# A graph network on one core: the last stage written out without a loop, its moments kept per tile, roots and reciprocals taken for four tiles at a time

## What is computed

```python
x = _layernorm(x + _L0_gnn_ref(x, ..., edge_index), axis=-1)
x = _layernorm(x + _L1_gnn_ref(x, src, dst, ...), axis=-1)

# in _L1_gnn_ref, at its end:
S = agg[:, :2 * F] @ (W1_s / np.sqrt(2 * F))
V = jnp.einsum('nmi,mc->nci', agg[:, 2 * F:8 * F].reshape(n, 2 * F, 3), W1_v) / np.sqrt(2 * F)
S = shifted_softplus(S)                    # softplus(x) - log 2
S = S @ (W2_s / np.sqrt(C))                # C = 128
V = jnp.einsum('nci,cd->ndi', V, W2_v) / np.sqrt(C)
return jnp.concatenate([S, V.reshape(n, 3 * C)], axis=1)

def _layernorm(x, axis=-1, eps=1e-05):
    m = jnp.mean(x, axis=axis, keepdims=True)
    v = jnp.var(x, axis=axis, keepdims=True)
    return (x - m) / jnp.sqrt(v + eps)
```

## Time and profile before

| | |
|---|---|
| time, median of 3 runs | 1854.98 us (1854.6 to 1856.04) |
| the profiled execution: time | 1854.7 us |
| its span in the profile | 1853.0 us |
| busy over the span: PE, DVE, ACT, POOL | 75%, 65%, 53%, 57% |
| granted clock of PE over the span, and in the tile turns of `touched` | 0.849, and 0.50 (1.2 GHz) |
| last POOL instruction of the kernel | starts 1846.41 us |

### The profile page before, as it was taken

One profiled execution on the slowest core, in us unless ns is written; L12 is line 12 of the kernel. 1 busy time (PEld: TensorE's weight loads), 2 busy tenths in 40 slices (PEclk: granted clock), 3 DMA queues, 4 the chain that ended last, 5 costly groups with the idle time before them and its releaser, 6 DMA issues. The chain is left out here.

```text
span 1853.0 us, 27588 instructions
## 1 busy us (share of the span) xinstructions
PE 1396.9 (75%) x8180; PEld 1204.7 (65%) x8180; DVE 1206.3 (65%) x3308; ACT 982.5 (53%) x1960; POOL 1048.5 (57%) x1095
## 2 busy tenths in 40 slices
PE   4669599999968999996699999353333239999833
PEld 4558488888856888885588888242232128888722
DVE  6575466666637777763699997464444239999865
ACT  3743144444425777762566664385656634444476
POOL 4773757777534787774423320577777744333236
PEclk8995699999987999998799999566655569999955
DMA  2000556666545766753555552888786532233112
GB/s 58 2 2 1 151 196 222 218 223 220 192 161 205 260 250 241 252 200 143 212 180 220 210 185 107 257 279 271 256 267 234 200 118 84 88 90 91 52 62 112
DMA packets 98920, 313.66 MB, mean 169 GB/s; under 512 B 34576, under 2 KB 36064, under 8 KB 98802
## 3 DMA queue, kind: packets, MB, share of 16 engines
q0 software_dynamic: 62720, 183.99, 29.5%
q1 hardware_dynamic: 36082, 128.24, 19.6%
HBM read 161.18 MB, written 156.39 MB: 171 GB/s over the span
## 5 line engine op out<-in xcount | busy, mean ns | idle before, releaser
L851 PE MATMUL ps_b<-yhi,whi 128*128 128x500 f32 x960 | 390.3, 407 | 8.6 <-DVE ylo L718 8.6
L851 PE MATMUL ps_b<-yhi,wlo 128*128 128x500 f32 x960 | 375.2, 391 | 0.0
L851 PE MATMUL ps_b<-ylo,whi 128*128 128x500 f32 x960 | 374.9, 390 | 0.0
L795 ACT COPY aggT<-ps_b 128x500 f32<-128x500 f32 x240 | 137.9, 574 | 347.1 <-PE ps_b L851 347.1
L747 DVE BATCH_NORM_STATS2 stat<-aggT 128x6 f32<-128x500 f32 x240 | 163.2, 680 | 200.4 <-ACT aggT L795 198.3
L635 POOL DMA_INDIRECT rows<-rows_out,node_at x160 | 187.0, 1169 | 118.3 <-ACT rows_out L800 82.7
L1068 PE MATMUL fin_ps_x<-ident,fin_X 128*127 128x128 f32 (+1 forms) x320 | 75.4, 405 | 176.9 <-DVE fin_xr L1000 163.4
L851 PEld LDWEIGHTS ps_b<-yhi,whi 128*128 128x128 f32 x960 | 182.5, 190 | 40.1 <-DVE ylo L718 9.1
L851 PEld LDWEIGHTS ps_b<-yhi,wlo 128*128 128x128 f32 x960 | 181.4, 189 | 37.8
L851 PEld LDWEIGHTS ps_b<-ylo,whi 128*128 128x128 f32 x960 | 182.4, 190 | 30.8
L1068 PEld LDWEIGHTS fin_ps_x<-ident,fin_X 128*127 128x127 f32 (+1 forms) x320 | 65.8, 298 | 192.8 <-DVE fin_xr L1000 169.2
(11 more groups left out here) (344 smaller groups left out, 3319.8 us busy)
## 6 DMA issues: line engine op xcount, KB each, us to landing
z<-aggT SPq DMA_DIRECT2D x60, 1000.0 KB, 5.3
X<-z SPq DMA_DIRECT2D x40, 1000.0 KB, 5.3
fin_X<-z SPq DMA_DIRECT2D x20, 1000.0 KB, 6.8
rows<-rows_out,node_at POOLq DMA_INDIRECT x160, 3.1
own_row<-in_L_gnn_W SPq DMA_DIRECT2D x2, 1024.0 KB, 10.6
others<-ord_nodeid,ord_place_node POOLq DMA_INDIRECT x80, 2.1
R<-in_x,node_at POOLq DMA_INDIRECT x80, 3.6
G<-rows,srci POOLq DMA_INDIRECT x80, 5.3
```

Of the source, the lines that this page charges most:

```text
L795: nc.scalar.copy(f.aggT[t % 2][:, j, :], f.ps_b[j % 2][:, 0:COLS]).then_inc(x["copied"], 1)
L851: o = nc.tensor.matmul(f.ps_b[j % 2][:, 0:COLS], w[:, c, j * P:(j + 1) * P], y[b % 2][:, c, :], start=(c == 0 and i == 0), stop=(c == C - ...
```

## The change

In `touched`, and nowhere else but for the sizes of its tiles:

- No loop: each engine's 40 turns are written out, with constant waits and slices.
- PE reads `l.sT` directly (L1467 and `l.hb` go), starts with the first of the four parts of the shifted sum and has four banks instead of two.
- DVE writes the moments of all 40 tiles to one tile `l.mv` (128 x 40 x 2) with no wait for a buffer; reciprocal and product are taken once for four tiles (`GS = 4`), after tile b with b % 4 = 1 of the next group. Each instruction has its wait right ahead of it.
- ACT takes the root of four tiles at once, one group ahead of the scalings.
- POOL reads the column of `l.row` directly (L1490 and `l.idx2` go).

```diff
-    RING = 8
+    RING, GS, parts = 8, 4, 4
+    NG, per = ET // GS, ET // parts
...
+    group = [slice(g * GS, (g + 1) * GS) for g in range(NG)]
...
         @block.scalar
...
-            act.wait_ge(s["plus"], parts)
-
-            def body(t):
-                if t.runs(3):
-                    b, q = t.block(3), t.slot(3, 2)
-                    ge(act, s["prod"], b - 1)
-                    nc.scalar.copy(l.hb[q][:], l.sT[:, bass.ds(P * b, P)]).then_inc(s["hcopy"], 1)
-                if t.runs(0):
-                    b, q = t.block(), t.slot(0, 2)
-                    act.wait_ge(s["aggr"], b + 1)
-                    nc.scalar.activation(l.std[q][:], l.mv[q][:, 1:2], ACT.Sqrt, bias=k.eps[:, 0:1]).then_inc(s["root"], 1)
-                if t.runs(-1):
-                    b, q, r = t.block(-1), t.slot(-1, 2), t.slot(-1, RING)
-                    act.wait_ge(s["nmr"], b + 1)
-                    ge(act, put[r], 16 * t.round(-1, RING))
-                    nc.scalar.activation(l.Y[r], x_row(b), ACT.Identity, scale=l.rstd[q][:], bias=l.nmr[q][:]).then_inc(s["done"], 1)
-            run(act, body)
+
+            def root(g):
+                act.wait_ge(s["aggr"], GS * (g + 1))
+                nc.scalar.activation(l.std[:, group[g]], l.mv[:, group[g], 1], ACT.Sqrt, bias=k.eps[:, 0:1]).then_inc(s["root"], 1)
+
+            root(0)
+            for g in range(NG):
+                if g + 1 < NG:
+                    root(g + 1)
+                act.wait_ge(s["nmr"], g + 1)
+                for b in range(GS * g, GS * g + GS):
+                    ge(act, put[b % RING], 16 * (b // RING))
+                    nc.scalar.activation(l.Y[b % RING], l.X[:, b, :], ACT.Identity,
+                                         scale=l.rstd[:, b:b + 1], bias=l.nmr[:, b:b + 1]).then_inc(s["done"], 1)
...
         @block.gpsimd
...
-                    ge(pool, s["idx2"], b + 1)
-                    ge(pool, s["done"], b + 1)
-                    ge(pool, put[r_next], 16 * t.round(0, RING))
-                    if t.runs(0):
-                        nc.gpsimd.tensor_copy(l.idx2[r_next][:], l.row[:, bass.ds(b + 1, 1)]).then_inc(s["idx2"], 1)
-                    pool.indirect_dma_start(out_dram, bass.IndirectOffsetOnAxis(ap=l.idx2[r][:, 0:1], axis=0), l.Y[r], None,
-                                            bounds_check=m.N - 1, oob_is_err=False).then_inc(put[r], 16)
...
+            for b in range(ET):
+                ge(pool, s["done"], b + 1)
+                pool.indirect_dma_start(out_dram, bass.IndirectOffsetOnAxis(ap=l.row[:, b:b + 1], axis=0), l.Y[b % RING], None,
+                                        bounds_check=m.N - 1, oob_is_err=False).then_inc(put[b % RING], 16)
...
         @block.tensor
...
+            for b in range(ET):
+                pe.wait_ge(s["plus"], b // per + 1)
+                ge(pe, s["ysum"], b - 3)
+                nc.tensor.matmul(l.ps[b % 4][:, 0:P], l.sT[:, P * b:P * (b + 1)], l.W2s[:], start=True, stop=True).then_inc(s["prod"], 1)
...
         @block.vector
...
+            def scales(g):
+                dve.wait_ge(s["root"], g + 1)
+                nc.vector.reciprocal(l.rstd[:, group[g]], l.std[:, group[g]]).then_inc(s["rec"], 1)
+                dve.wait_ge(s["rec"], g + 1)
+                nc.vector.scalar_tensor_tensor(l.nmr[:, group[g]], l.mv[:, group[g], 0], -1.0, l.rstd[:, group[g]],
+                                               ALU.mult, ALU.mult).then_inc(s["nmr"], 1)
...
+            for b in range(-2, ET):
+                if b + 2 < ET:
+                    dve.wait_ge(s["prod"], b + 3)
+                    nc.vector.tensor_tensor(l.X[:, b + 2, 0:P], l.X[:, b + 2, 0:P], l.ps[(b + 2) % 4][:, 0:P], ALU.add).then_inc(s["ysum"], 1)
+                if 0 <= b + 1 < ET:
                     dve.wait_ge(s["ysum"], b + 2)
...
+                    ge(dve, s["aggr"], b)
+                    nc.vector.bn_stats(l.st[(b + 1) % 2][:], l.X[:, b + 1, :]).then_inc(s["stats"], 1)
+                if b >= 0:
                     dve.wait_ge(s["stats"], b + 1)
...
+                    nc.vector.bn_aggr(l.mv[:, b, :], l.st[b % 2][:]).then_inc(s["aggr"], 1)
+                    if b % GS == 1 and b >= GS:
+                        scales(b // GS - 1)
+            scales(NG - 1)
```

More of the change, by code:

```diff
@@ L1431, in touched @@
 def touched(m, k, l, out_dram):
-    nc, ET = m.nc, m.ET
+    nc, ET, D = m.nc, m.ET, m.D
     mag = l.rows[:, 0:m.EPAD]
-    names = ("mag", "exp", "log", "pos", "plus", "vec", "hcopy", "prod", "ysum", "stats", "aggr", "root", "rec", "nmr", "done", "idx2")
+    names = ("mag", "exp", "log", "pos", "plus", "vec", "prod", "ysum", "stats", "aggr", "root", "rec", "nmr", "done")
     s = {n: m.sem(f"tch_{n}") for n in names}
-    RING = 8
+    RING, GS, parts = 8, 4, 4
+    NG, per = ET // GS, ET // parts
     put = [m.sem(f"tch_put{r}") for r in range(RING)]
-    parts = 4
     part = [slice(i * m.EPAD // parts, (i + 1) * m.EPAD // parts) for i in range(parts)]
[L1443 to L1447, removed]
+    group = [slice(g * GS, (g + 1) * GS) for g in range(NG)]
     with nc.Block() as block:
@@ L1518, in _, with plus @@
             dve.wait_ge(s["pos"], parts)
-            for i in range(parts):
+            def plus(i):
                 dve.wait_ge(s["log"], i + 1)
@@ L1522, in _ @@
                                                ALU.add, ALU.add).then_inc(s["plus"], 1)
-            def body(t):
-                b = t.block()
-                if t.runs(1):
+            def scales(g):
[4 more added lines that the diff above has]
+                                               ALU.mult, ALU.mult).then_inc(s["nmr"], 1)
@@ L1528, in body @@
+            for i in range(parts):
+                plus(i)
+            for b in range(-2, ET):
[3 more added lines that the diff above has]
+                if 0 <= b + 1 < ET:
                     dve.wait_ge(s["ysum"], b + 2)
-                if t.runs(0):
+                    ge(dve, s["aggr"], b)
+                    nc.vector.bn_stats(l.st[(b + 1) % 2][:], l.X[:, b + 1, :]).then_inc(s["stats"], 1)
+                if b >= 0:
@@ L1530, in body @@
                     dve.wait_ge(s["stats"], b + 1)
[L1531 to L1547, removed]
-                    nc.vector.scalar_tensor_tensor(l.nmr[q][:], l.mv[q][:, 0:1], -1.0, l.rstd[q][:], ALU.mult, ALU.mult).then_inc(s["nmr"], 1)
@@ L1549, in _ @@
-            run(dve, body)
+                    nc.vector.bn_aggr(l.mv[:, b, :], l.st[b % 2][:]).then_inc(s["aggr"], 1)
+                    if b % GS == 1 and b >= GS:
+                        scales(b // GS - 1)
+            scales(NG - 1)
 class Bag:
@@ L1698, in build @@
             l.dot = m.sb("l_dot", [P, P])
-            l.st, l.mv = two("st", [P, 6]), two("mv", [P, 2])
-            l.std, l.rstd, l.nmr = (two(n, [P, 1]) for n in ("std", "rstd", "nmr"))
+            l.st, l.mv = two("st", [P, 6]), m.sb("l_mv", [P, ET, 2])
+            l.std, l.rstd, l.nmr = (m.sb(f"l_{n}", [P, ET]) for n in ("std", "rstd", "nmr"))
             l.Y = [g[:, 4 * h:4 * h + 4, :].rearrange("p a b -> p (a b)") for g in l.msg + l.agg for h in range(2)]
```

5 lines of the change are left out of this document (removed).

## The result

The changed kernel takes 1842.83 us (median of 4 runs, 1841.96 to 1843.39) beside 1854.79 of the kernel before (1854.13 to 1856.04): a ratio of 0.9934, 95% interval 0.9917 to 0.9952, 12.0 us less. It was run again later beside 15 runs of the kernel before: 1844.14 (1842.79 to 1844.88) to 1854.54, 0.9945, 0.9931 to 0.9958, 10.4 us less.

A forecast was written before the change was run, and what follows sets the result against it. A ring of DVE, ACT's copy and PE paced the last stage, POOL following; afterwards POOL paces. 14.5 us gained by pace less 4.4 lost at the start took 1854.7 to 1844.6, by the median 1844.9 us; range 1843.3 to 1849.5.

The forecast's parts named there:

- The bound before: Last stage: DVE, ACT's copy and PE wait in a ring, 1.67 us per tile; POOL follows with room.
- POOL at 1.28 us per write afterwards: Last stage after the change: POOL's writes pace, 39 steps of 1.28 us make 49.9, 14.5 us gained by the pace.
- ring and DMA have room: Last stage: eight output tiles need 4.9 of the 10.2 us that eight writes take; DMA share rises to 0.43.
- The start: Last stage: scaling waits for the moments of tile 7, so first write at 1786.4 against 1781.99, 4.4 us lost.
- p: DVE's time per tile for add, bn_stats and bn_aggr, without the scales: bounds 0.89 and 1.17 us, 1.03 taken.
- the 0.78: Time in us from the end of ACT's first scaling to the start of POOL's first write in the last stage.
- DVE slower than its starts say: Rival, last stage: DVE takes about 1.35 us per tile and starves POOL by groups; 1851.9 us, chance 6%.
- POOL's instruction grows beside a denser DVE: Rival, last stage: POOL's write takes 1.17 us, 1.47 with issue, as in the layers; 1852.3 us, chance 6%.
- Slower, because the gap belongs to the wait: Rival, last stage: POOL's idle time before each write stays without the copy, pace 1.65 us; 1859.4 us, chance 4%.
- No effect: Rival, last stage: an unseen wait, say the four banks, keeps the ring closed; 1855 us, chance 2%.

The follow-up runs named there:

- loops_out: The kernel before with the last stage's 40 turns written out instead of a loop, nothing else changed: 1852.24 us, ratio 0.9987.
- out_nohb: The kernel before with turns written out, TensorE reading `l.sT` directly over four banks and starting earlier, POOL's index copy kept: 1844.68 us, ratio 0.9948.
- out_nopoolcopy: The kernel before with turns written out and POOL's index copy and its waits removed: 1852.39 us, ratio 0.9988.
- after_skip: The changed kernel with every place marked as skipped, so the last stage's writes carry no rows: 1844.27 us, ratio 0.9945.
- after_poolcopy: The changed kernel with POOL's index copy put back ahead of each write: 1846.18 us, ratio 0.9953 to the kernel before.
- after_ring4: The changed kernel with a ring of four output tiles instead of eight: 1843.82 us, ratio 0.9947 to the kernel before.
- after_stats2: The changed kernel with a second, unused bn_stats per tile on DVE: 1855.75 us, ratio 1.0007 to the kernel before.
- after_gs1: The changed kernel with groups of one tile, a root and a reciprocal for each: 1838.41 us, ratio 0.9918 to the kernel before.

## Why the prediction missed its range by 0.5 us

**The bound before** (a ring of DVE, ACT's copy and PE, POOL a follower): right. loops_out and out_nohb landed 0.6 and 1.0 us under their numbers, with the steps as expected, out_nopoolcopy gave nothing.

**POOL at 1.28 us per write afterwards:** right to the last digit that the profile gives, 49.9 us for 39 steps. That it holds with rows and with none (after_skip), that a copy adds 0.06 (after_poolcopy) and that ring and DMA have room (after_ring4, after_skip) came out as worked out.

**The start** is the term that was mis-sized. I had the first write 30.6 us after the stage's start (1786.4 less 1755.8), it came at 29.54: 4.4 us lost were forecast, 3.35 measured. The step that failed is the choice of p. The starts in the earlier trace rows gave 0.89, the one step with a wait 1.17, and I took the middle, 1.03, "since the new order has no wait ahead of the add but four waits per tile to issue". It was 0.88, with those waits in place. So waits that are already met cost DVE nothing here; the 1.17 held an idle time of 0.20 that came from waiting for the bn_aggr just ahead, and the new order has no such wait. Seven tiles at 0.15 too much are 1.05 us. Against that, a scaling to its first write took 0.93 us (1782.01 + 0.81 to 1783.75), not the 0.78 that I took from another stage in the earlier trace rows; the rest of the sum was right to 0.2.

**The range** had no term for the stages ahead of the change. With p at its lower bound the sum gave 1843.6, and the stage's 11.2 us off 1854.98 give 1843.8, inside the range: p alone does not carry the forecast out of it. The stage's 11.2 us off the medians beside which the changed kernel ran give 1843.6 and 1843.3; measured were 1842.83, 0.8 us less, and 1844.14, 0.8 us more. With the stage itself the same to 0.05 us, this is put down to the stages ahead. Only the profiled executions show them: they put the start of this stage anywhere within 2.3 us. Whether a first median lands 0.8 us to one side or the other is chance. A range for a median of a few runs has to include that spread, here about 1 us to each side.

**The rivals.** DVE slower than its starts say: wrong, it was as fast as them. The mechanism is real: after_stats2 shows it, with 0.59 us more per tile. POOL's instruction grows beside a denser DVE: wrong. Its ground was weak as well: where the 160 longer writes stand, DVE was busy for 58 to 72% of each 200 us (122.76, 115.83, 143.92 and 135.31, from 200 to 1000), no denser than the 67 and 73% of the tile turns before. What lengthened them stays open. Between 1776 and 1800 DVE was busy 23.80 of 24 us, and the writes of that stretch took 0.97 us except the first two, with 1.01 and 1.00. By the rule of the Trainium skill (SBUF — State Buffer, section Who interferes with whom) an operation with at most one input in SBUF and outside the two-port modes leaves GpSimd alone; the trace agrees for bn_stats, bn_aggr and an add with one input in PSUM. What the prediction left out of that section is that an operation with two inputs in SBUF contends with a GpSimd instruction that reads SBUF. The product `l_nmr<-l_mv,l_rstd` is such an operation; in after_gs1, which has one for every tile, the writes are 0.97 us too, but for the same first two. Slower, because the gap belongs to the wait: wrong, all gaps between writes are 0.30 or 0.31. The part of it that holds is the latency of 0.93 us ahead of the first write. No effect: wrong, the step fell from 1.652 to 1.279.

## What to carry to other kernels

Count the hand-over ring, not the busy shares: with three engines busy for two thirds to three quarters, cutting the ring at a copy of 0.29 us, with two more banks, was worth 7 us, and a copy on a waiting engine nothing. Once one engine paces, look at its first instruction: POOL's busy time plus its issue time gave the 39 steps to 0.1 us, and everything that delayed its first write was paid in full. Grouping small operations saved time on DVE, which had time, and delayed POOL, which had none. Within one engine, put each wait directly ahead of its instruction and give each small result its own place; here the two together were worth 6.5 us, and taking roots and reciprocals by four nothing.

## What I had not expected of the hardware

- An indirect DMA of 128 rows costs POOL 0.97 us and 0.30 of issue, with 2 KB rows or with none that are carried (after_skip, 1.282 us a step to 1.279); only the landing got shorter, 2.1 us in place of 2.6.
- DVE took 0.88 us for three operations whose durations add up to 0.26 + 0.69 + 0.17 = 1.12: each start comes before the end of the operation ahead, also across different operations and with waits between them that are already met. A wait for the operation just ahead costs differently by place: the add behind a turn's waits stood idle for 0.20 or 0.23 us (out_nohb), while the product, with a wait of its own for the reciprocal just ahead, started 0.16 us after it, 0.03 behind its end (out_nohb, after_gs1). What makes the difference isn't shown.
- The stages ahead, from the same source, took between 1754.2 and 1756.5 us in fourteen profiles, while the last stage of the changed kernel came out the same to 0.05 us in two.
